# The stages ahead of the first edge sum, the threshold search and the batch normalisation of a two-layer graph network

## What is computed

```python
xn = layernorm(x)
# L0 gnn, 4 layers, 4 relations:
inv_deg = 1 / max(count of edges with this destination and this type, 1)
h = einsum('ni,rio->rno', X, W)                    # the tables, one per relation
agg = segment_sum(h[etype, src] * inv_deg, dst)
X = elu(layernorm(agg + X @ root + bias)) + X
x = x + X + mix(xn)
# L0 ffn on the rows whose score is among the KK = 3124 highest
x = x + ffn(layernorm(x))
xn = layernorm(x)
# L1 gnn, 8 relations, and batch norm over all nodes:
agg = segment_sum(all_h[src, rel], dst)
out = (agg - mean(agg, 0)) * rsqrt(var(agg, 0) + eps) * gamma + beta
x = x + out + linear_attention(xn)                 # sums of products of keys and values
x = x + experts(layernorm(x))
```

## Time and profile before

| | us |
|---|---|
| median of 3 runs | 7477.67 |
| lowest and highest run | 7469.09, 7491.65 |
| the profiled execution, its own time | 7467.94 |
| its span in the trace | 7466.1 |
| `edge_tables` | 23 to 220 |
| `weights0` | 220 to 232 |
| `norm0` | 232 to 285 |
| tables of layer 0, to the first gather | 285 to 567 |
| `select` | 5018 to 5160 |
| `gnn1` | 5547 to 6606 |
| `batch_norm` | 6634 to 6787 |

### The profile page before, as it was taken

One profiled execution on the slowest core, in us unless ns is written; L12 is line 12 of the kernel. 1 busy time (PEld: TensorE's weight loads), 2 busy tenths in 40 slices (PEclk: granted clock), 3 DMA queues, 4 the chain that ended last, 5 costly groups with the idle time before them and its releaser, 6 DMA issues. The chain is left out here.

```text
span 7466.1 us, 90239 instructions
## 1 busy us (share of the span) xinstructions
PE 5299.9 (71%) x19104; PEld 3488.7 (47%) x19104; DVE 4222.2 (57%) x14685; ACT 2860.3 (38%) x7106; POOL 4218.9 (57%) x4274
## 2 busy tenths in 40 slices
PE   0397777777777767777767777774987766753498
PEld 0244444444444444444436666652444444442365
DVE  7305666657776766666656666654336666633322
ACT  0134444434444445555545555540223333311122
POOL 0007777767777767777757766640027777724111
PEclk9998999989998989999988888886997787876799
DMA  2344444444445444544443333321443333310000
GB/s 61 132 131 139 134 135 131 135 134 145 147 144 147 144 143 145 147 140 140 141 125 110 107 103 104 104 66 47 139 133 105 106 106 106 105 40 1 14 15 20
DMA packets 480199, 815.56 MB, mean 109 GB/s; under 512 B 89423, under 2 KB 343971, under 8 KB 479479
## 3 DMA queue, kind: packets, MB, share of 16 engines
q0 software_dynamic: 200480, 548.02, 26.0%
q1 hardware_dynamic: 279252, 262.52, 10.8%
HBM read 614.04 MB, written 196.16 MB: 109 GB/s over the span
## 5 line engine op out<-in xcount | busy, mean ns | idle before, releaser
L491 POOL DMA_INDIRECT gnn_msg<-tables,row x4165 | 4007.9, 962 | 1810.1 <-issue 748.6
L557 PE MATMUL bank<-gnn_msg,gnn_hot 128*128 128x256 f32 x8330 | 2641.6, 431 | 795.7 <-DMA gnn_msg<-tables,row 241.0
L557 PEld LDWEIGHTS bank<-gnn_msg,gnn_hot 128*128 128x128 f32 x8330 | 1605.2, 212 | 1741.0 <-issue 1432.0
L540 DVE TENSOR_TENSOR sums<-sums,bank 128x256 f32 x3332 | 1392.0, 418 | 1273.4 <-PE bank L557 893.2
L514 ACT ACTIVATE gnn_away<-iota,meta 128x128 f32<-128x128 f32 x1960 | 622.8, 389 | 485.3 <-PE bank L557 476.6
L660 PE MATMUL bank<-gnn_w,residual 128*128 128x512 f32 x1176 | 653.3, 640 | 179.4 <-DVE sums L628 179.1
L523 ACT ACTIVATE gnn_hot<-gnn_away,meta,less 128x128 f32<-128x128 f32 x1568 | 645.8, 482 | 13.1
L500 DVE TENSOR_SCALAR gnn_hot<-iota,meta 128x128 f32<-128x128 f32 x1764 | 632.7, 359 | 0.5 <-DVE sums L1505 0.5
L540 DVE TENSOR_TENSOR residual<-residual,bank 128x256 f32 x833 | 351.3, 422 | 366.6 <-PE bank L557 297.5
L134 POOL TENSOR_TENSOR ve<-mv,eps 128x7 f32<-128x7 f32 x28 | 5.7, 205 | 941.5 <-DVE mv L128 793.2
L677 ACT COPY residual<-bank 128x512 f32<-128x512 f32 x294 | 171.0, 581 | 781.5 <-PE bank L660 780.9
(11 more groups left out here) (394 smaller groups left out, 6552.8 us busy)
## 6 DMA issues: line engine op xcount, KB each, us to landing
tables<-residual SPq DMA_DIRECT2D x294, 256.0 KB, 2.4
gnn_msg<-tables,row POOLq DMA_INDIRECT x4165
tables<-residual SPq DMA_DIRECT2D x98, 512.0 KB, 2.9
tables<-gnn_msg SPq DMA_DIRECT2D x98, 256.0 KB, 2.1
residual<-first_norm_columns SPq DMA_DIRECT2D x98, 128.0 KB
residual<-first_rows SPq DMA_DIRECT2D x98, 128.0 KB, 3.0
first_norm<-state SPq DMA_DIRECT2D x1, 6272.0 KB, 20.7
first_rows<-residual SPq DMA_DIRECT2D x1, 6272.0 KB, 39.0
```

The costliest lines, as they stand in the source:

```text
L491: self.nc.gpsimd.indirect_dma_start(out=self.msg[:, s, :], out_offset=None, in_=table, in_offset=bass.IndirectOffsetOnAxis(ap=self.rows[:, ...
L540: self.nc.vector.tensor_tensor(at, at, self.sums(n, s), ALU.add).then_inc(self.added, 1)
L557: self.nc.tensor.matmul(self.sums(n, s), self.hot[:, s, :], self.msg[:, s, :], start=True, stop=True).then_inc(self.summed, 1)
```

## The change

Four parts.

1. `edge_tables`, `norm0` and the tables of the first layer become one stage, `edges_and_tables`, called inside `gnn0`. `weights0` comes ahead of it and runs while x is still loading; it stores its result itself. The state is normalised in place by ScalarE (Identity with a scale and a shift, which POOL makes) once SP has stored the group's rows of x, so that the copy to a stage is gone. The three products go to three banks of their own; ScalarE evicts all three, and VectorE adds the bias a group at a time. SP's list holds the records' store ahead of tile 17, the tile numbers' ahead of tile 33 and their reload ahead of tile 36. TensorE's list holds the edges' matmuls ahead of tiles 8, 26 and 36 to 42. The temporary arrays lie in rooms that are free at the time, so three waits guard them (`BUSY_FROM`, `RECORDS_FROM`, and the vectors' load).
2. `select` makes 16 rounds instead of 64. A round compares all 49 scores with 17 marks and narrows the interval 16 times.
3. The batch norm's sums move into `gnn1`: for each finished tile TensorE makes the column sums (into bank 0) and adds them to a row of bank 3, VectorE subtracts the tile's mean, ScalarE squares, TensorE sums the squares. `batch_norm` joins the 49 tiles' sums by their counts; the centring of `c.agg` stands behind POOL's start signal.
4. The key statistics are spread over slots 12 to 16.

The core of the diff:

```diff
+def edges_and_tables(nc, c, a, msg, hot, w, vecs, away, own_room):
+    RECORDS_AT, TILES_OUT_AT, TILES_IN_AT = 17, 33, 36
+    BUSY_FROM, RECORDS_FROM = NT - -(-(11 * EC + 1) // D), NT - -(-REL0 * EC // D)
+    PLANE_BANKS = [5 + b % 3 for b in range(SB)]
+    MEET_AT, COUNT_AT, PLANES_AT = 8, 26, 36
...
+                for to, of in ((e_dst, a["dst"]), (e_t4, a["edge_type_4"]), (e_src, a["src"]), (e_t8, a["edge_type_8"])):
+                    sp.dma_start(to, of.rearrange("(p n) -> p n", p=EP)).then_inc(s_in, 16)
...
+                for g in range(NG):
+                    sp.dma_start(rows_of(c.x_d, g), group(c.xn, g)).then_inc(s_kept[g], 16)
...
+                def prepare(n, g):
+                    k0, m = CH[n]
+                    act.wait_ge(s_pow, 4 * (g + 1))
+                    act.wait_ge(s_kept[g], 16)
+                    gate(act, c)
+                    for t in range(g * GT + k0, g * GT + k0 + m):
+                        sc.activation(state(t), state(t), ACT.Identity, bias=shift[:, t:t + 1], scale=rs[:, t:t + 1]).then_inc(s_nrm, 1)
...
+                def way_out(n, g):
...
+                            sc.copy(outs[:, o, :], c.bank[2 + j][:]).then_inc(s_out, 1)
+                        if t == BUSY_FROM:
+                            act.wait_ge(s_rec, 4 + 1)
+                        if t == RECORDS_FROM:
+                            act.wait_ge(s_recd, 32)
+                        act.wait_ge(s_root, t + 1)
+                        sc.copy(c.agg[:, t * D:(t + 1) * D], c.bank[4][:, 0:D]).then_inc(s_rooted, 1)
...
+                def bias(g):
+                    dve.wait_ge(s_rooted, (g + 1) * GT)
+                    gate(dve, c)
+                    x = group(c.agg, g)
+                    v.tensor_tensor(x, x, vecs[:, 2:3, :].to_broadcast([P, GT, D]), ALU.add).then_inc(s_bias, 1)
...
+                        if t == COUNT_AT:
+                            pe.wait_ge(s_below, NT + 1)
+                            mm(c.bank[5][:, 0:NT + 1], c.ones[0:EP, :], below[:], start=True, stop=True).then_inc(s_counted, 1)
+                        if 0 <= t - PLANES_AT < SB:
+                            b = t - PLANES_AT
+                            pe.wait_ge(s_pl, b + 1)
-    ROUNDS = 64
+    ROUNDS, WAYS = 16, 16
...
+                    v.tensor_scalar(mark[:, 1:WAYS], c.iota[:, 1:WAYS], width[:, 0:1], lo, ALU.mult, ALU.add).then_inc(s_mark, 1)
+                    dve.wait_ge(s_mark, i + 1)
+                    v.tensor_tensor(over[:], scores, marks, ALU.is_ge).then_inc(s_over, 1)
+                    dve.wait_ge(s_over, i + 1)
+                    v.tensor_reduce(counts[:], over[:], AX.X, ALU.add).then_inc(s_cnt, 1)
...
+class Moments1:
+    def columns(self, pe, r, n, t):
...
+        pe.wait_ge(c.edges.added, n * SLOTS)
+        gate(pe, c)
+        tile = c.agg[:, ds(t * D, D)]
+        mm(self.column, c.ones[:], tile, start=True, stop=True).then_inc(self.s_col, 1)
+        mm(self.totals, self.into_row(r), tile, start=False, stop=False)
...
+                self.nc.vector.scalar_tensor_tensor(self.cen, self.column, self.less[:, ds(t, 1)], self.c.agg[:, ds(t * D, D)],
+                                                    ALU.mult, ALU.add).then_inc(self.s_cen, 1)
...
 def batch_norm(nc, c, a, scale):
+                then(v.tensor_scalar(sums[:], c.bank[6][:, 0:D], 1.0 / N, None, ALU.mult))
+                dve.sem_inc(s_p, 1)
+                for g in range(NG):
+                    x = group(c.agg, g)
+                    v.tensor_tensor(x, x, mean[:].unsqueeze(1).to_broadcast([P, GT, D]), ALU.subtract).then_inc(s_cen, 1)
...
+                pool.wait_ge(s_p, 1)
+                nc.gpsimd.tensor_tensor(sums[:], sums[:], eps[:], ALU.add).then_inc(s_p, 1)
+                pool.wait_ge(s_p, 2)
+                nc.gpsimd.tensor_tensor(sums[:], sums[:], power[:], ALU.pow).then_inc(s_p, 1)
```

More of the change, by code:

```diff
@@ new lines, in edges_and_tables @@
+        plane, valid = late(SB, 4, P), late(SB, P)
+        e_t4, e_t8 = (cut_sums(EC)[0:EP].bitcast(I32) for _ in range(2))
+        ahead, same = [cut_sums(EC)[0:EP] for _ in range(REL0)], cut_sums(EC + 1)[0:EP]
+        behind_room = cut_sums(REL0 * EC)
+        behind = [behind_room[0:EP, r * EC:(r + 1) * EC] for r in range(REL0)]
+        e_rec = behind_room[0:EP].bitcast(I32).rearrange("p (n f) -> p n f", f=4)
+        meets = cut_away(4, P)[0:EP, :, 0:EP]
+        ends_row = cut_own(2, P)[0:EP, :, 0:EP]
@@ L279, in edge_tables @@
+        upper, lower = (cut_own(P)[0:EP, 0:EP] for _ in range(2))
         rec_d = c.rec_d
@@ L1998, in after @@
         def after(s):
-            if s == 13 and first:
+            if s == 12 and first:
                 dve.wait_ge(self.s_kv, i + 2)
@@ L2017, in gnn1 @@
+def gnn1(nc, c, wt, acc, pick, work, less):
     with Phase(nc, "gnn1") as ph:
@@ new lines, in _ @@
+                v.tensor_copy(sums[:], c.bank[3][:, D:2 * D]).then_inc(s_sums, 1)
+                then(v.memset(own[:], 0.0))
+                then(v.memset(eps[:], EPS))
+                then(v.memset(power[:], -0.5))
+                dve.wait_ge(s_turned, 1)
+                then(v.tensor_copy(rows[0:NT, :], c.bank[5][0:NT, 0:1]))
+                then(v.reciprocal(part[0:NT, :], rows[0:NT, :]))
+                dve.wait_ge(s_sums, 1)
+                then(v.tensor_copy(own[row:row + 1, :], sums[row:row + 1, :]))
@@ new lines, in _ @@
+                x = own[0:NT, :]
+                dve.wait_ge(s_mean, 1)
+                then(v.tensor_scalar(mean[:], c.bank[4][:, 0:D], 1.0 / N, None, ALU.mult))
+                then(v.scalar_tensor_tensor(x, sums[0:NT, :], part[0:NT, 0:1], mean[0:NT, :], ALU.mult, ALU.subtract))
+                then(v.tensor_tensor(x, x, x, ALU.mult))
+                v.tensor_scalar(x, x, rows[0:NT, 0:1], None, ALU.mult).then_inc(s_own, 1)
+                dve.wait_ge(s_apart, 1)
+                then(v.tensor_scalar(sums[:], c.bank[6][:, 0:D], 1.0 / N, None, ALU.mult))
```

686 lines of the change are left out of this document (350 added, 336 removed).

## The result

| | us |
|---|---|
| predicted | 7103, range 7065 to 7165 |
| the change, median of 4 runs | 7096.79 (7091.79 to 7101.07) |
| before, median of 4 runs | 7484.66 (7469.09 to 7494.38) |
| ratio | 0.9485, 95% interval 0.9472 to 0.9499 |
| the profiled execution of the change, its span | 7095.5 |

The change is 5.2% faster, and the median lies 6 us under the forecast. The sum hit, but not all of its terms did. Between the two medians lie 387.9 us, 13 more than forecast, and between the two profiled executions 370.6, 4 less: the kernel before alone ranges over 25 us. This table cuts both spans at the same five places: the first gather of all, the search's maximum over the partitions, the first and the last gather of the last edge sum, and POOL's first product with the scale in `mix1_main`.

The account below looks back on a forecast made before the run. No engine is near full; the kernel is a row of stages with different limits. Joint stage -239, search -52, batch normalisation -89, last edge sum +5 make -375 from 7477.67: 7103 us, range 7065 to 7165.

Parts of the forecast that it names:

- (a): Before the joint stage: mixer weights are loaded behind x, turned and their store waited for; the stage begins at about 40.
- (b): Start of the joint stage: loads, x's first group stored at +22, normalisations and turning; products begin 28.7 in, at 68.7.
- (c): Joint stage, the 49 tiles' products on TensorE: 254.6 us instead of 267.3, ending at 323.3.
- the -10 for the wait for a bank: Joint stage, 49 tiles: three banks take away the 0.2 us a tile waits for a bank, 10 us gained.
- the +6: Joint stage, 49 tiles: the edges' own matmuls come in on TensorE, 6 us more.
- the 19.7: Joint stage, 49 tiles: TensorE's one wait for the stores of x and xn, 19.7 us, is dropped whole.
- the 3 for stalls: Joint stage, 49 tiles: 3 us for all stalls from the added waits, ends 0 and 35.
- The second rival: Joint stage goes in steps: TensorE waits at tile 36, ScalarE for places, or x comes late; 35 to 60 more; chance 0.13.
- The two terms for the centring: Batch normalisation: centrings held by POOL delay its start by 4.7 us and leave five behind the power, 10.2 us.
- the other case: Batch normalisation: the centring runs freely beside POOL's power; 15 us more gained, 7088; chance 0.15.
- +5: Last edge sum: bodies keep POOL's pace; only the end is bare, with two sums, last square and wider closing passes: +5 us.
- the third rival: Last edge sum: bodies grow as new pieces tie three engines in a ring; 1 us per body is 49, 7152; chance 0.05.

Follow-up runs that it names:

- norm_ahead: The change, with ScalarE normalising the chunk after next tile by tile behind each tile's eviction; first gather at 322.7 us instead of 339.2, span 7075.6.
- search_64: The change with the search of 64 halvings put back; search stretch 526.6 us instead of 472.3, span 7156.7.

## Why the prediction was right

- **(a) and (b), up to the first product.** 68.3 for 68.7, with two misses that cancel: the stage began at 37.6 for 40, and the way to the first product took 30.7 for 28.7. The rows of x were in their store when ScalarE wanted them, 23.1 into the stage for 22.
- **(c), the 49 tiles: the step that failed.** 265.8 us for 254.6. Two terms of its sum were wrong. The first is the -10 for the wait for a bank. It came from two tiles that end 4.47 apart, and these are among the stage's last seven. In the chunks before those, tiles inside a chunk end 4.42 apart, and the first of a chunk takes 4.32:

```profile
307.40 0.42 DVE L1505 TENSOR_TENSOR sums<-bank,gnn_vecs 128x256 f32 x1 [4.00 <-PE bank L1357]
311.82 0.42 DVE L1505 TENSOR_TENSOR sums<-bank,gnn_vecs 128x256 f32 x1 [4.00 <-PE bank L1357]
```

  Tiles with no turning and no fall in them last 4.40 on average before and 4.31 in the change, so the 49 gained about 4.5 us, not 10. The second is the condition that stood beside the +6: "if TensorE's fast clock holds as it did in this window". It doesn't. Six falls of about 1.7 are 10 us, against the 1.4 of before, and they come with the waits. Over the eight profiles that have these twelve waits, 37 of the 96 had a fall, each beginning from 0.4 us before the wait's end to 1.4 behind it. The runs with three falls have their first gather at 332.7 to 333.0, those with five or six at 336.3 to 339.2; and with the waits cut to 1.05 us there was none. So a wait of 2.0 to 2.5 us was priced at its own length, and cost up to its length and 1.7 again; why one wait had a fall and the next had none stays open. The rest is small: the 19.7 went as forecast, the waits ahead of turnings grew by 10.2 for 8, the edges' matmuls lengthened the tiles by about 4.2 for 6, and the 3 for stalls didn't come. Together that is 11.7 too much, against 11.2 measured.
- **What VectorE does meanwhile.** The forecast's claim that it waits for TensorE, not TensorE for it, held, but by another count: the counts were ready at 200.0 (212.99 - 12.96), not at 182. The 17.89 us that VectorE waits at tile 8 had been left out, where the added waits were listed. It did no harm only because TensorE came late itself, at 266.9 for about 250: five falls had cost it 8.5 by then, and the forecast reckoned these arrivals with 5.0 a tile, where its own sum gives 254.6 / 49 = 5.2 and the trace 5.5. That the two are level at tile 36 was right to a microsecond (265.9 against 266.9), the two 19 and 17 us later than forecast, and norm_ahead shows what it was worth: a TensorE that comes earlier waits there, 6.06 us. The second rival (0.13) was as near as the forecast said.
- **The search.** -55 for -52, within the scatter of 4 us of its stretch; the round 4.35 for 4.4. search_64 gives the same back, +54.3.
- **The batch normalisation.** The sums ahead of the power fell from 138.6 to 35.0 us behind the last copy of the edge sum, 104 for 104. The two terms for the centring were wrong: +4.7 and +10.2 became 0 and 0, with 1.7 more of the power. The step was the reading of the earlier trace rows: a hold by a product was taken for a hold by any POOL instruction. The forecast had said that the trace has no row for this pair, and gave the other case 0.15; by the runs it was the one that came. The Trainium skill, in "SBUF — State Buffer", section "Who interferes with whom", has the second of two such instructions blocked until the first ends. The products show that in both directions, and the addition of 0.72 us did it too (the first centring took 0.58 longer); the power, an instruction with two operands of the same kind, doesn't, and there the measurement decides.
- **The last edge sum.** +5 for an end of about 6, and bodies of 21.3 still. But "neither this nor the spreading of the key statistics changes the body" treats as two small things what is one exchange: the sums took 82 us of TensorE's time over (111.0 to 29.2), and only the spreading keeps it from falling behind POOL. Without it the third rival (0.05) comes true for 28 us of its 49.
- **The total.** -375 forecast, -370.6 in the profiled pair. Each large term came within 14 us; that the sum is right within 6 us is luck: 11 too much gain at the joint stage, 12 too little at the edge sum's end and the batch normalisation, 3 too little at the search, and +8 from two stretches that scatter.

## What to carry to other kernels

When two chains are laid side by side, price each hand-over wait of the bound engine by its length and by what its clock does behind it, and move the helper's work one step earlier, where that engine is idle anyway. Then look at who becomes late next: here halving twelve waits brought a new one of 6 us with a fall of the clock, 10 us in all, until the meeting points were moved as well. And before an instruction is hidden beside another engine's, ask whether the pair itself is in a trace: the form of both decides, and the cheapest way out may be to drop the long one, as 12 short steps of 5.1 us in all did with a power of 42.9. And take a pace from the middle of a stage: its last tiles, 4.47 apart, stood for 49 that were mostly 4.42 and 4.32 apart, and half of a forecast gain of 10 us was not there.

## What the runs showed of the hardware

- A POOL power of 128x256 (41.27 us) lets VectorE's two-operand and two-scalar instructions through and gets 1.67 us longer with seven centrings beside it, no more with 28 small instructions added; a POOL product of 128x1792 (3.17 alone) and a VectorE subtraction of the same shape (2.01 alone) take turns, 4.83 and 4.99 each. The power costs as much as 57 additions of its shape (0.72).
- TensorE's clock can fall to 1.2 GHz for 3.4 us about the end of an idle time of only 2.0 to 2.5 us in an otherwise busy stage, in 37 of 96 cases over eight profiles, three to six a run; by gaps of 1.05 us it fell in none of the three runs that have them, by those of 2.2, 4.1 and 6.1 us that came in their place it did.
- Two executions of a kernel with nothing changed differed by 14 us in one stretch of 4460, while the whole span agreed within 0.15%.
